# A first image's chain on VectorE, a table of steps for images 1 to 3, and GpSimd's scalings behind pow

## The reference

```python
def _gn(v, G=32, eps=1e-05):     # 32 groups of one channel
    return (g - m) / sqrt(var + eps)

def _L0_conv_ref(x, w1, b1, fscale, conv_bias):
    avg = x.mean(axis=(2, 3))
    dyn = avg @ w1.T + b1
    wk = sigmoid(dyn).reshape(b * c, 1, K, K)
    y = depthwise_conv(x, wk) + conv_bias
    return (x - y) * fscale * x + y

x = x + _L0_conv_ref(_gn(x), ...)
```

## Time and profile before

| | us |
|---|---|
| median of 3 runs | 266.01 (265.41 to 266.79) |
| the profiled execution | 265.87 |
| its span | 263.9 |
| around the span | 2.0 |

### The profile page before, as it was taken

How to read it: one execution, slowest core, us unless ns; L and a number is a source line. 1 busy time by engine, 2 the same in 40 slices (tenths; PEclk the granted TensorE clock), 3 DMA queues, 4 the chain that set the end, 5 groups by cost and what they waited for, 6 DMA issues and landing times.

```text
span 263.9 us, 9720 instructions
## 1 busy us (share of the span) xinstructions
PE 235.7 (89%) x3872; PEld 187.7 (71%) x3872; DVE 231.7 (88%) x552; ACT 211.1 (80%) x389; POOL 227.6 (86%) x259
## 2 busy tenths in 40 slices
PE   0069998989999999989999999999999999999991
PEld 0046875858788786878787887678787878888770
DVE  2886799999999999999999999899999999756655
ACT  2158789797898989797998989697989989899520
POOL 1261579899899999999999999999999999999982
PEclk9999999999999999999999999999999999999997
DMA  7999904696959989797979799797989733444476
GB/s 259 421 422 429 383 4 180 212 401 255 362 236 366 365 280 392 253 390 306 368 288 361 295 366 354 287 386 247 361 325 362 281 160 160 183 181 181 183 290 247
DMA packets 10413, 77.73 MB, mean 295 GB/s; under 512 B 1280, under 2 KB 1408, under 8 KB 2688
## 3 DMA queue, kind: packets, MB, share of 16 engines
q1 hardware_dynamic: 10368, 77.12, 75.8%
HBM read 39.37 MB, written 37.75 MB: 292 GB/s over the span
## 4 chain that ended last, share of the span: by engine, by line
PE 58%; DVE 23%; issue 10%; DMA 3%; ACT 2%; SPq 1%; POOL 1%; DVEq 0%; ACTq 0%; POOLq 0%
PE conv_ps L435 37%; PE conv_ps L441 13%; DVE outs L582 9%; DVE pieces L531 8%; DVE taps L549 4%; PE dyn_ps L419 3%; DMA w1s<-w1r 3%; PE dyn_ps L427 2%; PE conv_ps L497 1%; DVE taps L556 1%; ACT xs L686 1%; ACT linear L722 1%; DVE row_stats L538 1%; PE dyn_ps L404 1%; SPq L314 1%
## 5 line engine op out<-in xcount | busy, mean ns | idle before, releaser
L435 PE MATMUL conv_ps<-xs,taps 64*64 64x448 f32 x1536 | 219.9, 549 | 6.9 <-DVE outs L582 4.3
L852 POOL TENSOR_TENSOR outs<-outs,linear 128x1152 f32<-128x1152 f32 x63 | 166.1, 2647 | 1.0 <-DVE outs L582 0.7
L582 DVE SCALAR_TENSOR_TENSOR outs<-xs,beta,conv_ps 128x576 f32<-128x576 f32 x128 | 102.8, 805 | 20.3 <-PE conv_ps L435 19.6
L435 PEld LDWEIGHTS conv_ps<-xs,taps 64*64 64x64 f32 x1536 | 101.7, 133 | 26.6 <-issue 14.0
L441 PE MATMUL conv_ps<-xs,taps 64*64 64x128 f32 x1536 | 114.3, 272 | 0.6 <-issue 0.6
L722 ACT ACTIVATE linear<-xs,slope 128x576 f32<-128x576 f32 x128 | 109.0, 854 | 3.0 <-POOL outs L852 3.0
L531 DVE BATCH_NORM_STATS2 pieces<-xs 128x6 f32<-128x64 f32 (+1 forms) x256 | 102.2, 447 | 6.0 <-DMA xs<-x 6.0
L441 PEld LDWEIGHTS conv_ps<-xs,taps 64*64 64x64 f32 x1536 | 94.2, 133 | 9.3 <-issue 2.4
L686 ACT ACTIVATE xs<-xs,shift 128x594 f32<-128x594 f32 x128 | 99.2, 778 | 0.0
L809 POOL TENSOR_TENSOR inv_std<-numbers,minus_half 128x8 f32<-128x8 f32 x16 | 26.4, 1649 | 4.8 <-ACT dev_mean L692 4.6
L549 DVE TENSOR_TENSOR taps<-dyn_ps,tap 128x1512 f32<-128x1512 f32 (+1 forms) x19 | 27.8, 1477 | 0.0
(11 more groups left out here) (59 smaller groups left out, 142.0 us busy)
## 6 DMA issues: line engine op xcount, KB each, us to landing
xs<-x SPq DMA_DIRECT2D x30, 1188.0 KB, 11.2
out<-outs SPq DMA_DIRECT2D x30, 1152.0 KB, 5.2
xs<-x SPq DMA_DIRECT2D x4, 594.0 KB, 6.0
out<-outs SPq DMA_DIRECT2D x3, 576.0 KB, 2.8
out<-outs SPq DMA_DIRECT2D x2, 288.0 KB, 2.6
cst<-const SPq DMA_DIRECT2D x1, 275.5 KB, 6.9
w1s<-w1r SPq DMA_DIRECT2D x1, 144.0 KB, 6.8
gates<-gate SPq DMA_DIRECT2D x1, 8.0 KB, 7.0
```

The source lines that it names most:

```text
L435: return nc.tensor.matmul(tile(i, g, taken)[:, START:BANK], taps[given, i % 2, at:at + HALF], xs[given, i % XBUFS, g, 0:PAIRED, 1 + shift: ...
L582: nc.vector.scalar_tensor_tensor(out=outs[:, i % OBUFS, g].rearrange("p (k w) -> p k w", w=COLS), in0=xs[:, i % XBUFS, g, :, 1:1 + COLS], ...
L852: nc.gpsimd.tensor_tensor(tile, tile, linear[:, PAIR * k:PAIR * (k + 1)].rearrange("p g n -> p (g n)"), ALU.add).then_inc(out_ready, 1)
```

## The change

What it does, engine by engine:

- SP loads image 0 in 8 pieces instead of 4 (`FIRST_LOADS`).
- VectorE takes image 0's `count` (`first_count`), `second_moments` (`first_moments`) and `average_columns` (`first_averages`); ScalarE and GpSimd lose these. The band copy stands behind `rows(0)`, `rows(1)` between the first and the second pair of image 0's matrices. Before `product(0, 0)` there are three tiles of statistics of image 2 instead of five; those of images 2 to 4 are dealt out anew in images 0 and 1, with `rows(3)` behind `product(1, 3)`.
- TensorE's `keep_warm` has 176 columns and 128 rows; nine stand with the statistics of image 0, working on its first tile, and the others between image 0's steps. Image 1's mean, which was whole and ahead of the tiles, becomes halves at steps 1 and 2.
- Steps of images 1 to 3 come from tables on TensorE and ScalarE; from image 4 on they are where they were.
- GpSimd: `scales(j)` holds pow, the averages' columns and the scalings together, in the image before; `beta` and `slope` get three buffers (`SCALES`). From image 1 on `scaled_taps` of image i+1 stands between the first and the second of the moment steps of image i+2, which wait for that image's negative mean.
- `rows` drops a wait that the wait for `count` contains.

```diff
 CONV_TILES = 3
-WARM = 240
-
-START_AHEAD, AHEAD = 4, 6
...
+            MEAN = {1: (0, 1), 2: (0, 12), 3: (1, 11)}
+            SPREAD = {1: (0, 4), 2: (0, 15), 3: (1, 14)}
+            AVERAGES = {1: (0, 9), 2: (1, 7)}
+            DYNAMICS = {1: (0, 11), 2: (1, 9)}
+
...
             def chain(i, at):
-                j = i + 1
-                if j < B:
-                    late = 3 if j <= 2 else 0
-                    if at == 3 + late:
+                for j in range(i + 1, min(i + 3, B)):
+                    mean = MEAN.get(j, (j - 2, 9))
+                    spread = SPREAD.get(j, (j - 2, 13))
+                    dynamics = DYNAMICS.get(j, (j - 1, 5))
+                    if (i, at) == AVERAGES.get(j, (j - 1, 3)):
                         averages(j)
...
-            def keep_warm(count):
+            def keep_warm(weights, moving, count):
                 for _ in range(count):
-                    nc.tensor.matmul(conv_ps[:, CONV_TILES - 1, BANK:BANK + WARM], const_of("average")[0:HALF],
-                                     cst[0:HALF, 0:WARM], start=True, stop=True)
-
+                    nc.tensor.matmul(conv_ps[:, CONV_TILES - 1, BANK:BANK + WARM], weights, moving, start=True, stop=True)
+
+            first = xs[:, 0, 0].rearrange("p k w -> p (k w)")
+            pe.wait_ge(first_loaded[0], 16)
+            for g in range(GROUPS + 1):
+                at_least(pe, pieces_done, g)
+                keep_warm(first[:, 0:PARTS], first[:, 0:WARM], 1)
+            pe.wait_ge(consts_loaded, 16)
+            still = (const_of("average"), cst[:, 0:WARM])
             mean_whole(0)
+            keep_warm(*still, 1)
             spread_whole(0)
-            keep_warm(3)
-            pe.wait_ge(last_columns_set, 1)
+            keep_warm(*still, 4)
+            pe.wait_ge(r_ready, 1)
+            keep_warm(*still, 1)
             averages_whole(0)
+            keep_warm(*still, 1)
             dynamics_whole(0)
-            keep_warm(2)
-            mean_whole(1)
-            keep_warm(1)
+            keep_warm(*still, 2)
+            pe.wait_ge(sig_ready, 1)
+            keep_warm(*still, 1)
+            pe.wait_ge(tap_ready, 1)
+            keep_warm(*still, 1)
...
+            def first_count():
+                dve.wait_ge(pieces_done, GROUPS)
+                nc.vector.tensor_scalar(pieces[:, 0, :, 1], pieces[:, 0, :, 1], const_of("counts"), None,
+                                        ALU.mult).then_inc(counted_ready, 1)
+
...
             for g in range(GROUPS):
                 bn(0, g)
             dve.wait_ge(consts_loaded, 16)
+            first_count()
+            rows(0)
             nc.vector.tensor_copy(band_ps, const_of("band")).then_inc(constants_set, 1)
-            rows(0)
             nc.vector.tensor_copy(avg_cols[:, TAPS * C:], const_of("spread")[:, TAPS * C:]).then_inc(last_columns_set, 1)
+            first_moments()
             dve.wait_ge(neg_f_ready, 1)
             nc.vector.reciprocal(inv_neg_f[:], neg_f).then_inc(inv_ready, 1)
-            for g in range(GROUPS):
+            for g in range(4):
                 bn(1, g)
+            first_averages()
+            for g in range(4, GROUPS):
+                bn(1, g)
+            dve.wait_ge(tap_ready, 1)
+            last_column(0)
+            first_matrices(0, 1)
             rows(1)
-            first_matrices()
-            for g in range(START_AHEAD):
+            first_matrices(1, PAIRS)
+            for g in range(3):
                 bn(2, g)
...
                 if i == 0:
-                    for g in range(START_AHEAD - 1):
-                        bn(2, START_AHEAD + g)
+                    product(0, 0)
+                    bn(2, 3)
+                    for g in range(1, 5):
+                        bn(2, 3 + g)
                         product(0, g)
-                    bn(2, GROUPS - 1)
-                    product(0, 3)
                     rows(2)
                     bn(3, 0)
-                    product(0, 4)
+                    product(0, 5)
                     bn(3, 1)
-                    product(0, 5)
-                    bn(3, 2)
                     matrices(1)
                     product(0, 6)
+                    bn(3, 2)
+                    product(0, 7)
                     bn(3, 3)
-                    product(0, 7)
-                    for g in range(4, AHEAD):
-                        bn(3, g)
+                elif i == 1:
+                    for g in range(4):
+                        product(1, g)
+                        bn(3, 4 + g)
+                    rows(3)
+                    product(1, 4)
+                    bn(4, 0)
+                    product(1, 5)
+                    bn(4, 1)
+                    matrices(2)
+                    product(1, 6)
+                    bn_ahead(4, 2, 4)
+                    product(1, 7)
+                    bn_ahead(4, 4, AHEAD)
...
             turn_weights()
-            count(0)
...
+            COPY_STATS = {1: (0, 2), 2: (1, 1)}
+            COPY_AVERAGES = {1: (0, 4), 2: (1, 4)}
+            COUNT = {2: (0, 5), 3: (1, 5)}
+            SIGMOID = {1: (0, 6), 2: (1, 6)}
+            MEAN = {1: (0, 0), 2: (0, 7), 3: (1, 7)}
...
+            def second_moments(j, taps_too):
                 pool.wait_ge(rows_done, j + 1)
                 pool.wait_ge(neg_mean_ready, j + 1)
                 nc.gpsimd.tensor_tensor(moments[:, 0], row_stats[:, j % 2, :, 0], neg_mean_of(j),
                                         ALU.add).then_inc(dev_ready, 1)
+                if taps_too:
+                    scaled_taps(j - 1)
...
             def scales(j):
+                pool.wait_ge(zstats_copied, 2 * (j + 1))
+                nc.gpsimd.tensor_tensor(inv_std[:, j % 2], numbers[:, j % 2, VAR], minus_half[:], ALU.pow).then_inc(r_ready, 1)
                 n = numbers[:, j % 2]
                 r = inv_std[:, j % 2].unsqueeze(1).to_broadcast([PARTS, 2, GROUPS])
+                pool.wait_ge(r_ready, j + 1)
+                if j > 0:
+                    nc.gpsimd.tensor_tensor(avg[:], dev_mean[:], inv_std[:, j % 2], ALU.mult).then_inc(avg_ready, 1)
                 nc.gpsimd.tensor_tensor(n[:, G1:GP + 1], factors[:], r, ALU.mult).then_inc(g1_ready, 1)
+                if j > 0:
+                    pool.wait_ge(avg_ready, j + 1)
+                    nc.gpsimd.tensor_tensor(avg_cols[:, 0:TAPS * C].rearrange("p (a g) -> p a g", g=GROUPS),
+                                            const_of("spread")[:, 0:TAPS * C].rearrange("p (a g) -> p a g", g=GROUPS),
+                                            avg[:].unsqueeze(1).to_broadcast([PARTS, TAPS * SLOTS, GROUPS]),
+                                            ALU.mult).then_inc(avg_cols_ready, 1)
                 pool.wait_ge(g1_ready, j + 1)
                 nc.gpsimd.tensor_tensor(roots[:], n[:, VAR:G1 + 1], r, ALU.mult).then_inc(roots_ready, 1)
-                nc.gpsimd.tensor_tensor(slope[:, j % 2], n[:, GP:CB + 1], shift[:, j % 2], ALU.subtract).then_inc(gain_ready, 1)
+                nc.gpsimd.tensor_tensor(slope[:, j % SCALES], n[:, GP:CB + 1], shift[:, j % 2], ALU.subtract).then_inc(gain_ready, 1)
                 pool.wait_ge(roots_ready, j + 1)
-                nc.gpsimd.tensor_tensor(beta[:, j % 2], roots[:, 0], inv_neg_f[:], ALU.mult).then_inc(beta_ready, 1)
+                nc.gpsimd.tensor_tensor(beta[:, j % SCALES], roots[:, 0], inv_neg_f[:], ALU.mult).then_inc(beta_ready, 1)
             def scaled_taps(j):
```

157 lines of the change are left out of this document (67 added, 90 removed).

## The result

The changed kernel takes 264.71 us (median of 19 runs, 262.07 to 265.84), the kernel before 265.82 (19 runs, 264.82 to 266.79): a ratio of 0.994, with an interval of 0.9921 to 0.9959. The forecast was 261.8. The execution that was profiled took 262.07 us (span 260.2): the lowest of its 19, and the only kind of execution that the forecast described. Most of the others lose up to 3.8 us against it, and where they lose them is the main subject of what follows.

The account below looks back on a forecast made before the run. VectorE was taken to set 14.44 us an image (14.0 work, 0.4 waits with TensorE) behind a 29.78 us start. −4.8 at p(0,0), partly given back in images 0 and 1, left −4.15: 265.87 to 261.7, stated as 261.8, range 259.9 to 265.0.

Parts of the forecast that it names:

- The level: TensorE in the start: at 2.4 GHz averages and dynamics halve, first conv at 20.7 us; at 1.2 GHz, 23.0.
- largest term: Start up to the first product of image 0: 25.0 us instead of 29.78, −4.8, resting on TensorE's high level.
- B: Rival: TensorE stays low until its first tiles, p(0,0) at 27.7, p(3,0) some 2.0 early; 263.9 us, chance 0.24.
- Aggregates, spread, pow, averages: Image 0's chain in the start: 10.8, 12.9, 14.1 and 17.15 us, the averages 1.2 earlier than before.
- the −0.7: First loads in eight pieces: image 0's statistics end near 10.5 us instead of 11.2.
- Images 0 and 1: VectorE, with 9 and 11 tiles of statistics, takes 15.1 and 16.6 us for these images.
- plus the 0.4 of waits: VectorE's waiting in each of images 0 and 1, added to its work to give 15.1 and 16.6 us.
- covered by the lead: TensorE's new waits (0.3, 1.5, 1.2) hidden by three buffers of `conv_ps`, 4.3 us of lead; 3.0 if uncovered.
- rival D: The tables cost more: waits at steps 11 and 14 and late additions uncovered; 264.9 us, chance 0.10.
- the main case: The whole kernel with TensorE's high level at the first tiles and new waits covered: −4.15, 261.8 us, chance 0.50.
- Worth nothing from image 3 on: GpSimd's new order cuts its period from 14.56 to about 14.2 us; VectorE and TensorE keep 14.44.
- E: Rival: tap values behind the negative mean delay the matrices in each of 13 later images; 268.9 us, chance 0.06.

Follow-up runs that it names:

- look_b: The changed kernel unaltered, profiled again (third trace); 265.44 us.
- pool_back: The changed kernel with GpSimd's order of the kernel before from image 2 on; 266.52 us, ratio 0.9991 to the kernel before.
- dense_warm: The changed kernel with its nine early warm-up products 240 columns wide instead of 176; 264.58 us, ratio 0.9955.
- high_warm: dense_warm with more warm-ups behind the mean and the spread and ahead of the averages and dynamics; 262.15 us, ratio 0.9855.
- lean: warm_pool with the first image in eight loads; 263.24 us, ratio 0.989.
- pool_chain: both_edits with image 0's moments and averages back on GpSimd; 262.07 us.
- late_mean3: The changed kernel with image 3's mean and spread at later steps and GpSimd's image-2 tap values ahead of image 3's moments; ratio 0.9858.
- warm_only: The kernel before with new warm-up products alone (240 columns in the loads, more behind them); 262.82 us, ratio 0.9878.
- warm_pool: warm_only with the changed kernel's GpSimd order from image 2 on; 262.06 us, ratio 0.985.
- lean_count: lean with image 0's count on VectorE ahead of the aggregates and the band copy behind them; 261.34 us, ratio 0.9845.
- both_edits: The changed kernel with high_warm's warm-up products and late_mean3's places of image 3's statistics; 262.08 us, ratio 0.9852.
- look_a: The changed kernel unaltered, profiled again (second trace); 262.73 us.
- mid_warm: The changed kernel without the first five of its nine early warm-up products; 264.72 us, ratio 0.9932.
- old_warm: The changed kernel with the warm-up products of the kernel before; 268.37 us, ratio 1.0104.
- new_pool: The kernel before with the changed kernel's GpSimd order and three scale buffers from image 2 on; 266.58 us, ratio 1.0009.

## Why the prediction was right, and where it failed

Two steps failed, the level's and the one on the waits of images 0 and 1.

**The level.** The mechanism was right, and the prediction said that its largest term, 4.8 us at p(0,0), rested on it; the step that failed is the one that made it a case with a chance of 0.50 against B's 0.24, as if one of the two held for the kernel. It holds for an execution. In the profiled one p(0,0) came at 24.84 (forecast 25.0) and the first four records of the tile took 0.97 us together; in look_b and pool_back the first two took 1.01. Nor was B's price right: it had p(0,0) at 27.7, p(3,0) 2.0 early and 263.9 us. In pool_back's trace, which is B's course, p(0,0) came at 27.17 but p(3,0) at 76.06, 0.75 later than before. In look_b they came at 26.43 and 75.32, and without its pause the time would be 264.4: the same waits behind p(0,0) ate the rest.

The section of the Trainium skill that the prediction named ("TensorE: Matmul & The Clock Gate", "What's actually happening") also says that the moment of the change differs from run to run of one kernel, which the prediction left out. The traces agree, and the moments lie 13 us apart: high at 11.6 us in one execution, near 17 in two others, near 25 in pool_back, with the same instructions up to there. The same section lets an idle array fall back. In look_b and dense_warm the clock fell behind pauses of 0.6 to 1.0 us, in high_warm, with pauses up to 0.45, it didn't; in the profiled execution of lean it didn't behind one of 1.73 either.

**Aggregates, spread, pow, averages:** 11.13, 13.50, 14.65, 17.38 against 10.8, 12.9, 14.1, 17.15. The second group of statistics waited 0.85 us for its load, which the −0.7 had spread evenly, and the mean's hand-overs took 0.2 more. Of the 0.97 us that the averages gained, the moved moments and averages have little: pool_chain has 0.16 us between the two chains. The rest came with the loads, the count and the aggregates' place ahead of the band copy. Tap values 19.81 (19.6 to 19.9) and conv 20.85 (20.7): right.

**Images 0 and 1:** 16.24 and 18.03 against 15.1 and 16.6, 2.57 us too little. The statistics tiles were counted rightly; the term that was mis-sized is "plus the 0.4 of waits". VectorE waited 2.9 us from p(0,0) to p(3,0), all of it in images 0 and 1, not 0.8; the other 0.5 is its work, 14.94 and 16.45 us where 14.7 and 16.2 were taken. The waits at the means, spreads and averages were seen one by one (0.3, 1.5, 1.2) and taken as "covered by the lead" of three buffers of `conv_ps`; TensorE waited 0.3, 0.6 and 1.8 in two, and they were not covered: VectorE's five waits for `conv_ps` in these images add up to 2.4 us. It is rival D's mechanism. That TensorE has no three tiles of lead, because VectorE's own product is what frees the buffer, is argued and not shown; only the wait of 0.94 us was taken away by an edit (late_mean3). The 2.57 us, less the 0.57 that image 2 took less (13.87 for 14.44) and the 0.16 of p(0,0), make p(3,0) 1.8 us later than forecast: D and the main case were no alternatives.

**GpSimd:** additions at 29.62, 33.84, 37.16, 42.66 and then 51.82 (forecast 29.7, 33.9, 37.3, 42.8, 50.2); the last is 1.6 us late by the 3.07 for the negated mean. "Worth nothing from image 3 on" holds for the kernel before as far as its times tell, and is wrong for kernels whose images come at 14.44 without a pause: 1.5 us in pool_back's trace against after's, 0.7 in warm_only's against warm_pool's. The prediction had the numbers, 14.56 against 14.44 and 0.93 us of slack (82.03 to 82.96), and didn't multiply the difference by the images.

**Later images:** 14.44 without exception in the profiled execution, and no matrices behind late tap values (E): right. The pauses of about 1 us that come in some executions were not in the sum.

So 261.8 was met by the profiled execution (262.07) by two errors that cancel, +1.8 at p(3,0) and, on the other side, 1.4 us that the kernel before took longer from there to its end (188.58 for 187.19). That it was met is luck. The median was missed by 2.9 us. In look_b the level cost 2.3 us and the pause 1.05, so these two can make such a miss; how they divide over the executions without a trace is known in part only (see the end).

## What to carry to other kernels

Where a start rests on TensorE's high level, look at more than one execution: a kernel's times that spread more than those of the kernel before are the sign, and record durations of the first matmuls tell which way an execution went. Size warm-ups for the high level, so that they leave no pause once it has come, and start them as soon as data is there; warm-ups that just filled the chain at the low level left pauses at the high one, and the level fell again in look_b and dense_warm. And before moving work for an earlier first product, find the engine that is busy nearly all the time from there to the steady part: here only VectorE's idle time was to be had, and lean_count, with one instruction moved (the count) and one reordered, has p(3,0) at 72.12 where both_edits, with the moved chain and the tables, has 72.60. And where one engine's period is longer than the kernel's, multiply the difference by the images: slack that looks ample in one image is gone some images later.

## What the runs showed that was not expected

**The same warm-ups, another moment.** In look_a TensorE ran 18 warm-up records from 3.62 us on, 7.64 us with no pause in the profile, and was low until after 16.9; in look_b a like stretch with a pause of 0.27 had raised it by 11.6. In pool_back, with a pause of 0.21, it was low until 25. With 240 columns instead of 176 the level was high by 14 us in all eight kernels profiled so.

**The page's clock row is not the whole of it.** In before the granted clock stands at 1.00 from the first slice on, while the first tile's records take 978 ns; only a fall behind a rise shows as 0.50. At a start, durations are what to read.

**The pause of TensorE** that the profile puts to issue (images of 15.1 to 16.1 us, one of numbers 8 to 12) is in before, look_a, look_b, mid_warm, old_warm and new_pool, and in none of the other eleven traces. The profile's DMA queue q8, which it calls "instruction", brings 30 or 31 loads of 16 KB in each execution. In all six traces the pause stands behind the longest time between two of them, 13.0 to 13.9 us (in look_a from 191.1 to 204.6), and TensorE goes on 1.3 to 1.4 us after the late load has landed. This suggests that TensorE had run out of instructions. It is a coincidence in six traces and no experiment, and what held the load up is open; both_edits and pool_chain have stretches of 13.1 and 12.6 us without a load, near 60 us, and no such pause. The 26 runs of high_warm, both_edits, warm_only, warm_pool and lean_count spread by 0.6 us at most in each kernel, so none of them seems to have it.

**How the executions of after divide** is known in part. Five of the 19 have a mean granted clock of 0.981 to 0.983 and take 265.04 to 265.82 us: they resemble look_b (0.979, 265.44), whose level fell. The other 14 have 0.993 or more and take 262.07 to 265.84, and there the clock doesn't tell a late first rise from an early one (pool_back, low until 25, has 0.999), nor the pause.
